# Order of side work in the feed-forward pairs of a fused attention and mixture kernel: silu before routing, later transpositions, remainders moved between VectorE and GpSimd

## The chip, the cores and the metric

The kernel runs on one core of a Trainium2 chip. The metric is the device time of one execution in microseconds (us); lower is better. Five engines have queues of their own: PE (TensorE, matrix products and transpositions), ACT (ScalarE), DVE (VectorE), POOL (GpSimd) and SP (here it only issues DMAs). Each works through its queue in order and waits on semaphores that the others raise.

## The reference

The input x is 2 x 1024 tokens of width 128, in float32. Four layers follow one another, each added to x behind a layer norm:

```python
x = x + attn_a(layernorm(x))   # 16 heads of differential attention, an rms norm per head, a projection
x = x + ffn(layernorm(x))
x = x + attn_b(layernorm(x))   # heads of 8, energies summed over positions, a softmax over 16, a projection
x = x + ffn(layernorm(x))      # the same weights as the first
```

with this feed forward, of 64 experts and one shared one:

```python
shared = silu(xf @ Ws_up) @ Ws_down
aff = xf @ centroids.T
_, idx = top_k(aff + expert_biases, 8)
w = sigmoid(take_along_axis(aff, idx)); w = w / (sum(w) + 1e-8)
cw = zeros(T, 64).at[rows, idx].add(w)
h = silu(einsum('td,edf->etf', xf, W_up))
routed = einsum('etd,te->td', einsum('etf,efd->etd', h, W_down), cw)
```

All 64 experts are computed for all tokens; the gates `cw` are zero for those that a token has not chosen.

## The kernel before

**Attention.** The first attention fills some 650 us. It is cut into 256 quads (`quad(s)`, s from 0 to NQ - 1 = 255): PE computes four score tiles of 128 x 512 (L1324) and, one quad later, the weighted sums of values in two halves (L1351); ACT takes the exponential of every score tile (L863). DVE finds row maxima 12 quads ahead and is done with them 12 quads before the end. In the last quads, side work for the first chunk of the feed forward is put between: `SIDE[NQ - 12]` to `SIDE[NQ - 4]`.

**Feed forward.** Tokens are taken in chunks of 512; n = 0 to 3 is the first feed forward, n = 4 to 7 the second. A chunk is 17 steps: w = 0 to 15 is a pair of blocks, each with two experts on the partitions, w = 16 the shared expert alone. Here (n, w) names a step, and g = 17 n + w counts them. In every product a float32 operand is split into a high part and a remainder, and three products are summed (L1449 to L1451). Of a pair g:

- PE: `up(g)`, six products of XH, XL with WUH, WUL, into two banks of PSUM;
- ACT: `silu(g)` (L948), in place;
- DVE: `gated(g)` (L1098) multiplies by the gates and writes HF;
- ACT: `high(g)` (L941) rounds HF to HH;
- DVE or POOL: `low(g)` (L1106 or L775), the remainder HL = HF - HH;
- PE: `down(g)`, six products that add up over the whole chunk in one bank.

In one step the queues hold, in this order:

```python
# PE                      ACT                    DVE                     POOL
side((n, w))              side((n, w))           side((n, w))            side((n, w))
up(g)                     silu(g)                gated(g)                low(g - 1), if low_on_pool(g - 1)
down(g - 3)               high(g - 1)            low(g - 1), if not on POOL
```

`up(g)` uses the banks of `up(g - 2)` again and so waits for `gated(g - 2)`. At w = 3, ACT also empties the sum of the chunk before (`chunk_sum`, L958, ahead of `side`), and PE's `down` of the new chunk's first pair waits for that. Which engine does `low(g)` is a rule, `low_on_pool(g)`, from what the side work of step g + 1 is. 44 of the 136 remainders are on POOL.

`SIDE` is the table of the side work: for each step a list of stages, each of which has a part on PE and parts on other engines. For a chunk of the feed forward they are: `stats` (DVE, L992, then the root on POOL, L621 and following), `norm` (DVE, L1004, writes XC), `x_T` (PE, L1230, transposes XC; ACT, L909 and L910, copies it to XT and XH; POOL, L745, makes XL), `affinity` (PE, L1407; ACT, L888, copies it, then L916 takes the sigmoid; POOL adds the biases), `top` (DVE), `sum` (DVE), `gate_T` (PE, L1411; ACT or, in the attention's last quads, DVE, L1127, copies it to CWT). For `gate_T` of chunk n SP then writes the gates to DRAM (L566), and reads them back, repeated over 64 partitions, two DMAs of 256 KB for a pair, into three slots of GATE (L577). The second attention is side work of the first feed forward too: `x_T` of "b", then `gram`, `gram_k`, `q_k`, `energy`, `soft_exp`, `mix_T`, `v_mix`, `v_all`, one stage a step. Its result goes out to DRAM and back through SP (`mix_out`, L552, at (3, 1) and (5, 1); `mix_back`, L558, at (3, 3) and (5, 3)), and `out_b` at (3, 5) and (5, 5) needs it.

In ACT's `side`, the stage `affinity` is a copy, a load of the table for sigmoid, the sigmoid, and later a load of the table for silu; there are seven such places in the feed forward, at (0, 9), (1, 9), (2, 0), (3, 10), (3, 16), (5, 10) and (5, 16).

Of the kernel before, what the change touches and what calls it, by code (L numbers as in the profile page):

```python
# [20 lines left out]
NCH = TOK // BANK  # L21
# [111 lines left out]
def ring_order(names):  # L133
# [19 lines left out]
SIDE = {  # L153

    NQ - 12: [("heads_T", 0)], NQ - 11: [("proj", 0), ("stats", ("f", 0))], NQ - 10: [("norm", ("f", 0))],
    NQ - 8: [("x_T", ("f", 0))], NQ - 7: [("affinity", 0)], NQ - 6: [("top", 0)], NQ - 5: [("sum", 0)], NQ - 4: [("gate_T", 0)],

    (0, 2): [("heads_T", 1)], (0, 4): [("proj", 1), ("stats", ("f", 1))], (0, 6): [("norm", ("f", 1))],
    (0, 8): [("x_T", ("f", 1))], (0, 9): [("affinity", 1)], (0, 11): [("top", 1)], (0, 13): [("sum", 1)],
# [18 lines left out]
for n, b in ((2, 0), (4, 1)):  # L178
    c, f = 2 * b + 1, 2 * b + NCH
    also((n, 4), ("y_T", n - 1), ("stats", ("b", c)))  # L180
    also((n, 6), ("norm", ("b", c)))
    also((n, 7), ("x_T", ("b", c)))
    also((n, 8), ("gram", b))
    also((n, 9), ("gram_k", b))
    also((n, 10), ("q_k", b))
    also((n, 11), ("energy", b))
    also((n, 12), ("soft_exp", b), ("soft_mix", b))
    also((n, 13), ("mix_T", b))
    also((n, 14), ("v_mix", b))
    also((n, 15), ("v_all", 2 * b))  # L190
# [101 lines left out]
def hybrid_layer(nc, x, w_qkv, w_proj, b_proj, lam_q1, lam_k1, lam_q2, lam_k2, sub_w,  # L292
                 w_q, w_k, w_v, w_o, b_o, cent, e_bias, ws_up, ws_down, w_up, w_down, out):
    ctx = ExitStack()
    with ctx:
# [151 lines left out]
        def _(sp):  # L447
# [102 lines left out]
            def mix_out(b):  # L550
                sp.wait_ge(*evacuated(("v_all", 2 * b + 1)))
                sp.dma_start(mixed_d[b].rearrange("i d a j -> (d a) i j"), VP[:]).then_inc(mix_w[b], 16)  # L552

            def mix_back(b):
                sp.wait_ge(mix_w[b], 16)
                if b:
                    sp.wait_ge(*evacuated(("out_b", 1)))
                sp.dma_start(RT[:], mixed_d[b].rearrange("i d a j -> (i d) (a j)")).then_inc(mix_r[b], 16)  # L558
# [10 lines left out]
            for n in range(2 * NCH):  # L569
                sp.wait_ge(gate_w, 16 * (n + 1))  # L570
                gates = gate_d[n].rearrange("(w u h) t -> w h u t", u=2, h=2)
                for w in range(FULL):
                    k = n * FULL + w
                    if k >= GSLOTS:
                        sp.wait_ge(hf_ok, k - GSLOTS + 1)
                    for h in range(2):
                        sp.dma_start(GATE[E * h:E * (h + 1), k % GSLOTS, :, :],  # L577
                                     gates[w, h].partition_broadcast(E)).then_inc(gate_ld[k % GSLOTS], 16)
                    if (n, w) in ((3, 1), (5, 1)):
                        mix_out((n - 3) // 2)  # L580
                    if (n, w) in ((3, 3), (5, 3)):
                        mix_back((n - 3) // 2)
# [212 lines left out]
        def _(act):  # L795
# [169 lines left out]
            for g in range(2 * NCH * WIDES):  # L965
# [572 lines left out]
```

## Time and profile before

| | us |
|---|---|
| median of 3 runs | 1110.72 |
| lowest and highest of them | 1108.67, 1111.96 |
| the profiled execution | 1112.18 |
| its span, first to last instruction | 1110.4 |

| engine | busy us | share of the span |
|---|---|---|
| PE | 1013.9 | 91% |
| DVE | 963.0 | 87% |
| ACT | 891.8 | 80% |
| POOL | 515.6 | 46% |

The profile is of one execution. Its clock of PE is at one of two levels: 1.00 is full speed (2.4 GHz), 0.50 half (1.2 GHz). In a timeline each row is one instruction or several alike: start, duration, engine, line, operation, tiles, sizes, count, and in brackets how long the engine was idle before it and what ended that. A matmul's row is longer than its share of PE, since matmuls overlap: starts are what counts.

### The profile page before, as it was taken

The page shows a single profiled execution, that of the slowest core. Times are in us where ns is not written, and L with a number is a line of the kernel's source. Part 1 is how long each engine was busy: PE and PEld are TensorE (multiplying, and loading weights), DVE is VectorE, ACT ScalarE, POOL GpSimd, SP SyncE. Part 2 cuts the span into 40 slices and gives each one's busy share as a digit, 9 for nine tenths or more (in the row PEclk, how much of TensorE's full clock was granted, in tenths as well). Part 3 has the DMA queues.
Part 4 walks back from the last instruction along what each step waited for, and adds up shares of the span by engine and source line. Part 5 has one row for each costly group of instructions (what it writes and reads, how often), then busy time and mean ns, then how long its engine had stood idle before and what let it go on. Part 6 is the DMA issues. An engine that isn't in the chain of part 4 may idle for free.

```text
span 1110.4 us, 21656 instructions
## 1 busy us (share of the span) xinstructions
PE 1013.9 (91%) x8016; PEld 517.5 (47%) x8016; DVE 963.0 (87%) x1174; ACT 891.8 (80%) x1466; POOL 515.6 (46%) x905
## 2 busy tenths in 40 slices
PE   6389999999999999999999999998899889999997
PEld 3022222222222223232322337776678667777875
DVE  7799999999999999999999738888868986687665
ACT  5189999999999999999999868767576767677765
POOL 3353556455645554455446645364325441442332
PEclk9579999999999999999999979999999999999999
DMA  8911110011001110111010026755567465857773
GB/s 279 302 33 36 51 49 24 29 51 50 25 27 51 50 31 22 51 50 31 23 51 21 3 68 166 175 135 135 143 155 187 114 171 138 209 142 176 190 194 86
DMA packets 80473, 108.91 MB, mean 98 GB/s; under 512 B 23536, under 2 KB 33520, under 8 KB 80368
## 3 DMA queue, kind: packets, MB, share of 16 engines
q1 hardware_dynamic: 70752, 103.07, 35.0%
q10 hardware_dynamic: 9616, 4.46, 1.5%
q8 instruction: 64, 1.05, 0.4%
q14 instruction: 41, 0.34, 0.1%
HBM read 95.57 MB, written 11.93 MB: 97 GB/s over the span
## 4 chain that ended last, share of the span: by engine, by line
DVE 57%; PE 22%; ACT 7%; issue 6%; DMA 5%; POOL 2%; SPq 1%; ACTq 0%; DVEq 0%; POOLq 0%
DVE NEGMAX L1057 46%; PE PS L1449 6%; PE PS L1451 5%; PE PS L1450 5%; DVE HF L1098 3%; DVE XC L1004 3%; DMA GATE<-gate_d 2%; PE PS L1351 2%; DVE HL L1106 2%; ACT HH L941 2%; PE PS L1324 1%; ACT PR L863 1%; ACT PS L948 1%; DVE ln_st L992 1%; DMA shift_d<-SHT 1%
## 5 line engine op out<-in xcount | busy, mean ns | idle before, releaser
L1057 DVE TENSOR_REDUCE NEGMAX<-PS 128x1 f32<-128x1024 f32 x512 | 585.0, 1211 | 9.7 <-PE PS L1287 9.1
L863 ACT ACTIVATE PR<-PS 128x512 f32<-128x512 f32 x1024 | 539.5, 601 | 42.4 <-PE PS L1324 30.3
L1351 PE MATMUL PS<-PR,VG 128*32 128x256 f32 (+1 forms) x3840 | 324.8, 410 | 16.7 <-ACT PR L863 1.3
L1324 PE MATMUL PS<-QB,KB 32*128 32x512 bf16 x1024 | 261.4, 390 | 3.7 <-DMA QB<-shift_d 2.3
L1287 PE MATMUL PS<-KA,QA 32*128 32x512 bf16 x1024 | 204.6, 397 | 30.3 <-DVE NEGMAX L1057 22.6
L1098 DVE TENSOR_TENSOR HF<-PS,GATE 128x1024 f32<-128x1024 f32 x128 | 156.1, 1221 | 71.0 <-ACT PS L948 70.6
L948 ACT ACTIVATE PS<-PS 128x1024 f32<-128x1024 f32 x128 | 129.3, 1010 | 91.7 <-PE PS L1451 90.5
L1324 PEld LDWEIGHTS PS<-QB,KB 32*128 32x128 bf16 x1024 | 75.2, 91 | 242.4 <-ACT PR L863 140.5
L775 POOL TENSOR_TENSOR HL<-HF,HH 128x1024 fp32r<-128x1024 f32 (+1 forms) x44 | 99.1, 2254 | 169.9 <-ACT HH L941 169.6
L941 ACT ACTIVATE HH<-HF 128x1024 fp32r<-128x1024 f32 (+1 forms) x136 | 139.7, 1028 | 26.9 <-DVE HF L1098 25.6
L1351 PEld LDWEIGHTS PS<-PR,VG 128*32 128x32 f32 x3840 | 76.7, 108 | 131.5 <-issue 65.9
L1106 DVE TENSOR_TENSOR HL<-HF,HH 128x1024 fp32r<-128x1024 f32 x92 | 116.3, 1265 | 21.6 <-ACT HH L941 21.2
L1449 PE MATMUL PS<-XH,WUH 128*128 128x512 f32 x256 | 108.9, 425 | 12.3 <-DVE HF L1098 12.3
L1449 PE MATMUL PS<-HH,WDH 128*128 128x512 f32 x256 | 103.5, 404 | 5.2 <-ACT YS L958 2.3
L1451 PE MATMUL PS<-XH,WUL 128*128 128x512 f32 x256 | 102.2, 399 | 0.0
L1450 PE MATMUL PS<-XL,WUH 128*128 128x512 f32 x256 | 101.9, 398 | 0.0
L1451 PE MATMUL PS<-HH,WDL 128*128 128x512 f32 x256 | 101.4, 396 | 0.0
L1450 PE MATMUL PS<-HL,WDH 128*128 128x512 f32 x256 | 101.2, 395 | 0.0
L683 POOL TENSOR_TENSOR ORC<-OSB,MINUS 128x16 f32<-128x16 f32 x32 | 93.1, 2910 | 9.9 <-DVE OSB L1083 7.6
L649 POOL TENSOR_TENSOR SHP<-NEGMAX,ZERO 128x16 bf16<-128x16 f32 x32 | 7.0, 217 | 168.8 <-DVE NEGMAX L1057 168.8
L1287 PEld LDWEIGHTS PS<-KA,QA 32*128 32x128 bf16 x1024 | 48.3, 91 | 58.5 <-DVE NEGMAX L1057 45.2
L1449 PEld LDWEIGHTS PS<-XH,WUH 128*128 128x128 f32 x256 | 48.9, 191 | 29.1 <-DVE HF L1098 18.6
(187 smaller groups left out, 991.4 us busy)
## 6 DMA issues: line engine op xcount, KB each, us to landing
GATE<-gate_d SPq DMA_DIRECT2D x256, 256.0 KB, 4.1
QA<-q_stack SPq DMA_DIRECT2D x64, 128.0 KB, 2.6
QB<-q_stack SPq DMA_DIRECT2D x16, 256.0 KB, 3.0
KB<-k_stack SPq DMA_DIRECT2D x16, 256.0 KB, 3.0
KA<-k_stack SPq DMA_DIRECT2D x60, 64.0 KB, 2.4
q_stack<-PARTS SPq DMA_DIRECT2D x12, 256.0 KB, 4.4
k_stack<-PARTS SPq DMA_DIRECT2D x12, 256.0 KB, 4.5
RAWU<-in_L_ffn_W_up_dram ACTq DMA_DIRECT2D x4, 512.0 KB, 13.3
```

The source lines that it names most:

```text
L863: nc.scalar.activation(PR[:, s % PRING, r, :], PS[:, SCORE_BANK[n], :], ACT.Exp, scale=SCALE_A).then_inc(p_ready, 1)
L941: nc.scalar.activation(HH[:, k, 0:u, :], HF[:, k, 0:u, :], ACT.Copy).then_inc(hh_ok, 1)
L948: nc.scalar.activation(PS[:, z:z + 2, :], PS[:, z:z + 2, :], ACT.Silu).then_inc(silu_ok, 1)
L1057: nc.vector.tensor_reduce(NEGMAX[:, hs % 2, col:col + 1], PS[:, e:e + 2, :].rearrange("p b n -> p (b n)"), axis=AX_X, op=ALU.max, negate=T ...
L1098: nc.vector.tensor_tensor(HF[:, k, :, :], PS[:, z:z + 2, :], GATE[:, h % GSLOTS, :, :], op=ALU.mult).then_inc(hf_ok, 1)
L1106: nc.vector.tensor_tensor(HL[:, k, 0:u, :], HF[:, k, 0:u, :], HH[:, k, 0:u, :].bitcast(F32), op=ALU.subtract).then_inc(hl_ok, 1)
L1287: last = mm(PS[:, e + h, :], QA[lo:lo + STRIP, u, r // 2, nt * P:(nt + 1) * P], KA[lo:lo + STRIP, u, r // 2, :], start=True, stop=True)
L1324: mm(PS[:, SCORE_BANK[n], :], KB[strip, u, mt * P:(mt + 1) * P], QB[strip, u, half * BANK:(half + 1) * BANK], start=True, stop=True).then_ ...
L1351: last = mm(PS[STRIP * r:STRIP * (r + 1), 7, cols], VG[:, u, mt, r // 2, :], PR[:, s % PRING, r, cols], start=mt == 0, stop=mt == TB - 1 a ...
L1449: mm(dst, ah, bh, start=first, stop=False)
L1450: mm(dst, ah, bl, start=False, stop=False)
L1451: return mm(dst, al, bh, start=False, stop=last)
```

## The change

1. `SIDE`: `gate_T` of chunk 0 goes from quad NQ - 4 to NQ - 2.
2. `SIDE`: `x_T` of chunk 3 goes from (1, 16) to (2, 0), and its `affinity`, `top`, `sum` and `gate_T` one step later each.
3. `SIDE`: for "b" chunks 1 and 3, `x_T` goes from (n, 7) to (n, 8), n = 2 and 4, and the ten stages behind it one step later each.
4. ACT: the routing part (copy and sigmoid of `affinity`) comes behind `silu(g)`, before `high(g - 1)`.
5. `mix_out` and `mix_back` are stages of `SIDE` now, issued by ACT at (n + 1, 0) and (n + 1, 2), and no longer by SP.
6. `low_on_pool`: the remainder that falls at an `affinity` step is always POOL's, and the last five are all DVE's. From before to now (0, 8), (1, 8), (2, 0), (3, 9), (3, 15), (5, 9) and (5, 15) go from DVE to POOL, and (2, 2), (7, 14) and (7, 16) from POOL to DVE.

```diff
-    NQ - 8: [("x_T", ("f", 0))], ..., NQ - 5: [("sum", 0)], NQ - 4: [("gate_T", 0)],
+    NQ - 8: [("x_T", ("f", 0))], ..., NQ - 5: [("sum", 0)], NQ - 2: [("gate_T", 0)],
...
-    also((n, 7), ("x_T", ("b", c)))
-    also((n, 8), ("gram", b))
+    also((n, 8), ("x_T", ("b", c)))
+    also((n, 9), ("gram", b))
...
-    also((n, 16), ("v_all", 2 * b + 1))
+    also((n + 1, 0), ("v_all", 2 * b + 1), ("mix_out", b))
+    also((n + 1, 2), ("mix_back", b))
...
 def low_on_pool(g):
-    n, w = divmod(g + 1, WIDES)
-    return g >= POOL_BUSY and (works((n, w), DVE_SIDE) and not works((n, w), POOL_SIDE) or not works((n, w), POOL_SIDE) and w % 3 == 0)
+    here = divmod(g + 1, WIDES)
+    if not POOL_BUSY <= g < 2 * NCH * WIDES - 5:
+        return False
+    if works(here, ("affinity",)):
+        return True
+    return not works(here, POOL_SIDE) and (works(here, DVE_SIDE) or here[1] % 3 == 0)
...
-            def side(where):
+            def side(where, routing=False):
                 for item in SIDE.get(where, ()):
                     stage, arg = item
                     bank = side_bank(item) if item in SIDE_ITEM else None
+                    if routing != (stage == "affinity" and item not in TAIL_SIDE):
+                        continue
...
+                    elif stage == "mix_out":
+                        act.wait_ge(*evacuated(("v_all", 2 * arg + 1)))
+                        act.dma_start(mixed_d[arg].rearrange("i d a j -> (d a) i j"), VP[:]).then_inc(mix_w[arg], 16)
+                    elif stage == "mix_back":
+                        act.wait_ge(mix_w[arg], 16)
+                        if arg:
+                            act.wait_ge(*evacuated(("out_b", 1)))
+                        act.dma_start(RT[:], mixed_d[arg].rearrange("i d a j -> (i d) (a j)")).then_inc(mix_r[arg], 16)
...
                 side((n, w))
                 if g > 1:
                     silu(g)
+                side((n, w), True)
                 if g:
                     high(g - 1)
```

What the queues hold at three places. **PE, the attention's last quads** (L1411, now L1413, is the transposition of the first gates), before:

```order
L1324 MATMUL PS<-QB,KB 128x512 x2
L1411 MATMUL PS<-ident,SQ 64x128 x4
L1351 MATMUL PS<-PR,VG 32x256 x4
L1324 MATMUL PS<-QB,KB 128x512 x2
L1351 MATMUL PS<-PR,VG 32x256 x4
L1324 MATMUL PS<-QB,KB 128x512 x2
L1351 MATMUL PS<-PR,VG 32x256 x4
L1324 MATMUL PS<-QB,KB 128x512 x2
L1351 MATMUL PS<-PR,VG 32x256 x4
L1324 MATMUL PS<-QB,KB 128x512 x2
```

and now:

```order
L1326 MATMUL PS<-QB,KB 128x512 x2
L1353 MATMUL PS<-PR,VG 32x256 x4
L1326 MATMUL PS<-QB,KB 128x512 x2
L1353 MATMUL PS<-PR,VG 32x256 x4
L1326 MATMUL PS<-QB,KB 128x512 x2
L1353 MATMUL PS<-PR,VG 32x256 x4
L1326 MATMUL PS<-QB,KB 128x512 x2
L1353 MATMUL PS<-PR,VG 32x256 x4
L1326 MATMUL PS<-QB,KB 128x512 x2
L1413 MATMUL PS<-ident,SQ 64x128 x4
L1353 MATMUL PS<-PR,VG 32x256 x4
```

Both begin at the same pair of score tiles; four halves of weighted values with their scores now come ahead of the transposition.

**ACT, steps (0, 8) to (0, 10)** (PS<-PS is a silu, HH<-HF a high, SQ the routing), before:

```order
L948 ACTIVATE PS<-PS 128x1024
L941 ACTIVATE HH<-HF 128x1024
L888 ACTIVATE SQ<-PS 128x256
L916 ACT_TABLE_LOAD
L916 ACTIVATE SQ<-SQ 128x256
L948 ACT_TABLE_LOAD
L948 ACTIVATE PS<-PS 128x1024
L941 ACTIVATE HH<-HF 128x1024
L948 ACTIVATE PS<-PS 128x1024
```

and now:

```order
L949 ACTIVATE PS<-PS 128x1024
L942 ACTIVATE HH<-HF 128x1024
L949 ACTIVATE PS<-PS 128x1024
L879 ACTIVATE SQ<-PS 128x256
L909 ACT_TABLE_LOAD
L909 ACTIVATE SQ<-SQ 128x256
L942 ACTIVATE HH<-HF 128x1024
L949 ACT_TABLE_LOAD
L949 ACTIVATE PS<-PS 128x1024
```

The silu of the step goes ahead of the routing, and the table for silu is loaded again only behind the high.

**DVE, the last steps of chunk 7**, before:

```order
L1098 TENSOR_TENSOR HF<-PS,GATE 128x1024
L1106 TENSOR_TENSOR HL<-HF,HH 128x1024
L1098 TENSOR_TENSOR HF<-PS,GATE 128x1024
L1106 TENSOR_TENSOR HL<-HF,HH 128x1024
L1137 TENSOR_TENSOR X<-X,PS 128x512
```

and now:

```order
L1100 TENSOR_TENSOR HF<-PS,GATE 128x1024
L1108 TENSOR_TENSOR HL<-HF,HH 128x1024
L1100 TENSOR_TENSOR HF<-PS,GATE 128x1024
L1108 TENSOR_TENSOR HL<-HF,HH 128x1024 x2
L1108 TENSOR_TENSOR HL<-HF,HH 128x512
L1139 TENSOR_TENSOR X<-X,PS 128x512
```

Two remainders, of (7, 14) and (7, 16), stand on DVE that were POOL's.

## Rows read from the trace of the kernel before

**Rows 1.** Page, section 1: busy us (share) and instructions

```profile
PE 1013.9 (91%) x8016; PEld 517.5 (47%) x8016; DVE 963.0 (87%) x1174; ACT 891.8 (80%) x1466; POOL 515.6 (46%) x905
```

**Rows 2.** Timeline of chunk 7: two silus, and what PE waited for

```profile
1093.39 1.01 ACT L948 ACTIVATE PS<-PS 128x1024 f32<-128x1024 f32 x1 [0.81 <-PE PS L1451]
...
1096.17 1.01 ACT L948 ACTIVATE PS<-PS 128x1024 f32<-128x1024 f32 x1 [0.81 <-PE PS L1451]
```

**Rows 3.** Timeline of the last quads: ACT, then PE

```profile
641.72 5.35 ACT L863 ACTIVATE PR<-PS 128x512 f32<-128x512 f32 x10 [0.33 <-PE PS L1324]
...
647.65 1.03 PE L1411 MATMUL PS<-ident,SQ 128*64 128x128 f32 x4 [1.70 <-POOL SQ L760]
...
658.92 0.80 PE L1449 MATMUL PS<-XH,WUH 128*128 128x512 f32 x1
```

**Rows 4.** Windows: length, busy us (count) by engine, PE's clock, DMA share, GB/s

```profile
647.20:660.86 13.66, 13.21 (x77) 4.14 (x78) 0.68 (x1) 7.79 (x13) 8.79 (x19) 0.50 0.57 125
...
797.39:800.80 3.41, 3.41 (x11) 2.73 (x10) 0.63 (x1) 1.00 (x2) 0.86 (x1) 0.50 0.32 92
...
913.44:916.85 3.41, 1.62 (x9) 1.44 (x10) 2.78 (x3) 0.60 (x1) 2.60 (x2) 1.00 0.27 72
```

**Rows 5.** Timeline from the first gates to the first gated pair: DVE, SP

```profile
648.72 0.68 DVE L1127 COPY CWT<-PS 64x512 f32<-64x512 f32 x1 [1.91 <-PE PS L1411]
663.13 1.22 DVE L1098 TENSOR_TENSOR HF<-PS,GATE 128x1024 f32<-128x1024 f32 x1
...
651.69 0.61 SPq L577 DMA_DIRECT2D GATE<-gate_d  x1
```

**Rows 6.** Tile GATE, 648 to 672 us: landing of its 13 loads

```profile
DMA to landing us min/median/max: 3.5/4.3/6.2
```

**Rows 7.** Timeline of (2, 6) to (2, 8), then (4, 7): DVE and PE

```profile
793.73 3.16 DVE L1004 TENSOR_SCALAR XC<-X,ln_mv,ln_inv 128x128 f32<-128x128 f32 x4
...
797.03 0.77 PE L1230 MATMUL PS<-ident,XC 128*128 128x128 f32 x4 [3.52 <-DVE XC L1004]
...
803.56 0.48 PE L1449 MATMUL PS<-XH,WUH 128*128 128x512 f32 x1
...
915.23 0.63 PE L1230 MATMUL PS<-ident,XC 128*128 128x128 f32 x4 [3.51 <-DVE XC L1004]
```

**Rows 8.** Timeline of the end of chunk 7: POOL, DVE, PE

```profile
1098.22 4.62 POOL L775 TENSOR_TENSOR HL<-HF,HH 128x1024 fp32r<-128x1024 f32 x2 [5.94 <-ACT HH L941]
...
1099.91 1.78 DVE L1106 TENSOR_TENSOR HL<-HF,HH 128x1024 fp32r<-128x1024 f32 x1 [1.48 <-ACT HH L941]
...
1100.75 0.47 PE L1449 MATMUL PS<-HH,WDH 128*128 128x512 f32 x1 [1.13 <-POOL HL L775]
```

**Rows 9.** Timeline of (0, 9) and (0, 11): ACT, DVE, POOL

```profile
686.72 0.38 ACT L888 ACTIVATE SQ<-PS 128x256 f32<-128x256 f32 x1
...
688.40 0.42 ACT L916 ACTIVATE SQ<-SQ 128x256 f32<-128x256 f32 x1
688.84 1.28 ACT L948 ACT_TABLE_LOAD   x1
690.13 1.01 ACT L948 ACTIVATE PS<-PS 128x1024 f32<-128x1024 f32 x1
...
697.60 1.22 DVE L1098 TENSOR_TENSOR HF<-PS,GATE 128x1024 f32<-128x1024 f32 x1
...
700.05 2.41 POOL L775 TENSOR_TENSOR HL<-HF,HH 128x1024 fp32r<-128x1024 f32 x1 [1.55 <-ACT HH L941]
```

**Rows 10.** Timeline of (2, 3): PE behind the chunk's sum

```profile
781.56 0.50 PE L1449 MATMUL PS<-HH,WDH 128*128 128x512 f32 x1 [0.46 <-ACT YS L958]
```

**Rows 11.** Timeline of (5, 10): ACT

```profile
982.40 0.36 ACT L888 ACTIVATE SQ<-PS 128x256 f32<-128x256 f32 x1
...
985.81 1.01 ACT L948 ACTIVATE PS<-PS 128x1024 f32<-128x1024 f32 x1
```

**Rows 12.** Line L552, the mixed values to DRAM, issued twice by SP

```profile
DMA to landing us min/median/max: 4.1/4.1/4.2
```

More of the change, by code:

```diff
@@ L155 @@
     NQ - 12: [("heads_T", 0)], NQ - 11: [("proj", 0), ("stats", ("f", 0))], NQ - 10: [("norm", ("f", 0))],
-    NQ - 8: [("x_T", ("f", 0))], NQ - 7: [("affinity", 0)], NQ - 6: [("top", 0)], NQ - 5: [("sum", 0)], NQ - 4: [("gate_T", 0)],
+    NQ - 8: [("x_T", ("f", 0))], NQ - 7: [("affinity", 0)], NQ - 6: [("top", 0)], NQ - 5: [("sum", 0)], NQ - 2: [("gate_T", 0)],
     (0, 2): [("heads_T", 1)], (0, 4): [("proj", 1), ("stats", ("f", 1))], (0, 6): [("norm", ("f", 1))],
@@ L163 @@
     (1, 10): [("heads_T", 3), ("x_T", ("b", 0))], (1, 11): [("top", 2)], (1, 12): [("proj", 3), ("stats", ("f", 3))],
-    (1, 13): [("sum", 2)], (1, 14): [("norm", ("f", 3))], (1, 15): [("gate_T", 2)], (1, 16): [("x_T", ("f", 3))],
-    (2, 0): [("affinity", 3)], (2, 2): [("top", 3)], (2, 4): [("sum", 3)], (2, 6): [("gate_T", 3)],
+    (1, 13): [("sum", 2)], (1, 14): [("norm", ("f", 3))], (1, 15): [("gate_T", 2)],
+    (2, 0): [("x_T", ("f", 3))], (2, 1): [("affinity", 3)], (2, 3): [("top", 3)], (2, 5): [("sum", 3)], (2, 7): [("gate_T", 3)],
     (4, 1): [("top", 5)], (4, 3): [("sum", 5)], (4, 5): [("gate_T", 5)],
@@ L181 @@
     also((n, 6), ("norm", ("b", c)))
-    also((n, 7), ("x_T", ("b", c)))
-    also((n, 8), ("gram", b))
[L184 to L190, printed above, removed]
-    also((n, 16), ("v_all", 2 * b + 1))
+    also((n, 8), ("x_T", ("b", c)))
+    also((n, 9), ("gram", b))
+    also((n, 10), ("gram_k", b))
+    also((n, 11), ("q_k", b))
+    also((n, 12), ("energy", b))
+    also((n, 13), ("soft_exp", b), ("soft_mix", b))
+    also((n, 14), ("mix_T", b))
+    also((n, 15), ("v_mix", b))
+    also((n, 16), ("v_all", 2 * b))
+    also((n + 1, 0), ("v_all", 2 * b + 1), ("mix_out", b))
+    also((n + 1, 2), ("mix_back", b))
     also((n + 1, 4), ("y_T", n))
@@ L548, in _ @@
             rows_out = out.rearrange("b (n p) c -> p (b n) c", p=P)
[L550 to L558, printed above, removed]
             def store(c):
@@ L578, in _ @@
                                      gates[w, h].partition_broadcast(E)).then_inc(gate_ld[k % GSLOTS], 16)
[L579 to L582, printed above, removed]
                     if n > NCH and w == 9:
```

## The prediction

> **What bounds the kernel now.** I read the engines' shares first [rows 1]: four engines are busy half of the time or more and none always, so the stages have to be told apart. The reader is to see in it only that PE leads. The change touches nothing ahead of the last quads, so I went on to the timeline behind 640 us.
>
> In chunk 7, which has almost no side work, silus start 2.78 us apart and each waits for PE [rows 2]: twelve products, 0.232 each. That is PE's own pace, and ACT has 0.81 to spare in each pair. Of eight chunks of 16 pairs and one shared step (2.78 and 1.39, half the products) this makes 367 us; from the first product at 658.92 [rows 3] to the last pair's DVE work near 1101.7 [rows 8] there are 443. The 76 between are waits, and the question is which of them the change takes away and which it makes. I looked at every wait of PE over 1 us there.
>
> **The first gates (part 1).** In quad 252 PE comes to the transposition of the gates and sits idle 1.70 us, until POOL has them at 647.5 [rows 3]. Behind it PE's clock is 0.50 for 13.66 us [rows 4]: from 647.65 to the first product at 658.92, 11.27 for one transposition, seven halves of weighted values with their scores, and the start [rows 3]. Ahead of it the exponentials set the pace, ten in 5.35 us, so 0.535 each and 2.14 for a quad of four [rows 3]. Two quads later the gates are long there. PE then comes to the transposition at 645.95 + 2 x 2.14 = 650.2, and to `up(0)` at 645.95 + 3.5 x 2.14 + 0.6 for the transposition = 654.0, 4.9 earlier. But the gates themselves are later by 2.2: the copy to CWT ended at 649.40 and the first load was issued at 651.69 [rows 5]; its pair's second one, 0.6 behind, takes the median of 4.3 [rows 6], so it lands at 656.6, and now at 658.8. `gated(0)` started at 663.13 [rows 5]; silu is no limit (654.0 + 1.4 + 1.3 for the table), so it starts at 658.9. **Term: -4.2.** The wait that goes is followed by another, for GATE. Bounds: if the clock falls all the same, only the idle 1.7 is saved; if GATE were there, 4.9 and the half-speed loss in `up(0)`, 1.0: -1.7 to -5.9.
>
> **Transpositions behind norms (part 3).** At (2, 7) PE waits 3.52 for the norm, which DVE does from 793.73 to 796.89, late and long, and at (4, 7) 3.51 [rows 7]. Now step (2, 7) has no such wait: `up(2, 7)` and `down(2, 4)` fill 793.5 to 796.3, PE then transposes at 797.0, and `up(2, 8)` waits for `gated(2, 6)`, which ends 1.2 behind the norm: 798.1. With 1.4 for `up` and 1.4 for `down` it is 800.9, and the gram products take 1.7: `up(2, 9)` at 802.6. Before, `up(2, 8)` was at 803.56 [rows 7], `up(2, 9)` 3.0 later at 806.6. **-4.0.** A part of it is the clock: behind the wait PE ran at 0.50 for 3.41 us [rows 4], which costs half of that, 1.7, and PE idle only 0.7 and 0.5 should not bring it about. At (4, 7) the clock stayed at 1.00 through an idle time as long [rows 4], so the same sum gives **-2.4**. Bounds for both together: nothing but the clock, -1.7, or both whole waits and the clock, -8.7. The ten stages behind follow in the same order one pair later and cost the same.
>
> **The last remainders (part 6).** PE waits 1.13 for POOL, whose two remainders take 4.62 together; DVE's own between them is stretched to 1.78 [rows 8]. On DVE the remainder of (7, 14) can follow `gated(7, 15)` at 1098.4 and end at 1099.6, where PE had come to at about 1099.6. Those of (7, 15) and (7, 16), 1.2 and 0.7, then keep ahead of PE. **-1.1**, between -0.5 and -1.1.
>
> **Routing behind silu (parts 2, 4 and 6).** Before, routing took ACT from 686.72 to 690.13: copy, load, sigmoid, load, and the sigmoid's end at 688.82 is 1.31 ahead of the silu, that is one load of 1.28 [rows 9]. ACT's work is the same now; what is new is that `silu(g)` can't start before PE has ended `up(g)`, while routing could. At (0, 9), ACT is free at 686.7 and `up` ends at 687.8: 1.1 idle put in. Then silu to 688.8, copy, load, sigmoid to 690.9, high to 691.9, load, and silu (0, 10) at 693.15, where it was 692.0. `gated(0, 9)` gains 2.2 and PE only 0.45, for it had waited no more. `high(0, 8)` comes as before, but its remainder is now POOL's, 2.41 long [rows 9] for DVE's 1.22: ready 694.4, PE wanted it 693.4. `gated(0, 10)` is late by 0.75, and so, through `top`, is `gated(0, 11)`, which was at 697.60 [rows 9] and set PE there. **+0.8.**
>
> At (2, 1), where routing of chunk 3 now stands, it is dearer. It used to run at (2, 0), when ACT had nothing else. Now ACT comes late to (2, 3), where it must empty chunk 1's sum: from silu (2, 1), which by the same replay of the queues from (1, 14) on starts at 775.7, follow silu, routing without the last load 2.1, high, load 1.3, silu and high, four of them at 0.94, so the copy of the sum starts at 782.9 and ends 783.45; PE waited for it until 781.56 [rows 10]. That is 1.9, and DVE has one more remainder in its full stretch to (2, 6), that of (2, 2), +0.5. **+2.4.** The move of `x_T` itself brings nothing, since PE waited right behind it for `gated` too. At (5, 10) PE runs at half speed when ACT has its copy at 982.40 [rows 11], `up` ends at 983.9, and 1.5 of idle ACT are put in, all of which DVE, full until `gated(5, 12)`, hands on: **+1.6**. The other four have 0.5 idle or a norm of DVE in the same place: 0.2 each, **+0.8**. Together **+5.6**; bounds 0 (DVE's relief pays for it) and 2.4 in each of the seven, 16.8.
>
> For the table loads the row decides: no gap beside the 1.28. The Trainium skill (ScalarE: Activation LUTs, What ACT_TABLE_LOAD costs) has some 1.38 of drain more at each switch. By it routing ahead of the high would be 1.4 longer, and the sum 7 x 1.4 = 9.8 higher, +3.7. The rows of before have no place for it, so it gets no chance.
>
> **The two DMAs on ACT's queue (part 5).** Written at (3, 0) and read at (3, 2): the write lands 4.1 after issue [rows 12] and 5.6 lie between, so ACT does not wait; issuing hides in the 0.81 of a pair. 0; at most +1.5 if the write took 7.
>
> **Sum.** -4.2 - 4.0 - 2.4 - 1.1 + 5.6 = -6.1. The profiled execution took 1112.18, so it would take 1106.1; it lies 1.46 above the median of 1110.72, and against that the forecast is **1104.6**. A measurement of this kernel can tell some 0.3%, 3.3 us, from no change.
>
> **Rivals.**
> *A. Routing costs nothing.* DVE has seven remainders fewer in its full stretches, which may pay for later silus. For: `gated` comes 2.2 earlier at (0, 9). Against: DVE idles there, so relief is worth little. Price: -11.7 + 0.6 = -11.1, 1099.6.
> *B. The gates are late.* PE, idle before the first gates land, falls to half speed, or six loads at once take the longest landing, 6.2 for 4.3 [rows 6]. Then -4.2 becomes -1.7 and the sum -3.6 or less, say 1108. For: 13.66 us at 0.50 followed an idle 1.7 [rows 4]. Against: 3.5 idle at (4, 7) brought nothing.
> *C. Remainders on POOL hold up DVE's.* DVE's took 1.78 in place of 1.22 beside POOL's [rows 8]; at seven places 0.56 each, +3.9, gives -2.2, 1108.5. The Trainium skill (SBUF — State Buffer, SBUF: two separate sides) says it outright: GpSimd and a DVE operation with two SBUF inputs lock each other out for the whole instruction. The row agrees.
> *D. Slower: `down` behind routing.* At every routing step PE waits for POOL's remainder or the chunk's sum as at (2, 1), 2.4 in each of seven, 16.8, and falls to half speed at two of them, 2 x 1.7. Then +20.2 - 11.7 = +8.5, 1119. It decides from 1.7 per place upward. For: I found 2.4 and 1.6 at two. Against: three had little.
> *E. It does not do what it says*: the order of the queues shows it done; no chance of its own.
>
> **How the numbers follow.** Forecast 0.46, and within it 1101.5 to 1107.5; A 0.20, B 0.13, C 0.11, D 0.10. Slower by over 0.3%: D's most, 0.09. Faster: A, 0.38 of the forecast, 0.09 of B and C, so 0.67. The same: the rest, 0.24. The range takes in A and reaches up to B and C: 1098.5 to 1110.0, with D and the ends left out.
>
> **What would show it.** PE's clock stays at 1.00 from 645 to 657 and `gated(0)` starts near 659, released by GATE; no wait over 1 us at x_T in (2, 8) and (4, 8); none for POOL at the end; a new wait of PE of 2 to 3 us at (2, 3), for YS; silu (g + 1) at routing steps 1 us later against its neighbours. I am wrong if the clock falls in the last quads all the same, or if the seven places sum to under 2 or over 9 us.

## The result and the profile after

| | kernel before | changed kernel |
|---|---|---|
| median us, 16 runs each | 1111.62 (1106.88 to 1114.34) | 1108.68 (1106.24 to 1111.91) |
| ratio | 1 | 0.9973, interval 0.9961 to 0.9984 |
| profiled execution us (span) | 1112.18 (1110.4) | 1111.91 (1110.0) |

The ratio makes 3.0 us less (1.8 to 4.3), where 6.1 less was forecast; the range held the time. It is just inside 0.3%, the forecast's bound of "the same". The profiled execution of the changed kernel was the slowest of its 16, so the two spans differ by 0.4 only. A second profile of it, e12, has a span of 1104.4, and a second one of the kernel before, e11, has 1109.4. What follows leans on both pairs. Two single runs, one of e1 at 1465 us and one of e4 at 2873 us, took far longer than all others and stand in no ratio.

Page of the changed kernel, section 1, for [rows 1]:

```profile
PE 1011.8 (91%) x8016; PEld 519.5 (47%) x8016; DVE 958.6 (86%) x1170; ACT 891.6 (80%) x1466; POOL 521.5 (47%) x909
```

Seven subtractions have gone from DVE to POOL and three back, four in all (1174 and 905 before). The shares tell nothing else; the places do.

**The last quads and the first gates.** Timeline of the changed kernel, PE, then SP's queue and DVE (start, us, engine and operation, in brackets the idle time before it and what ended it):

```profile
651.53 0.63 PE L1413 MATMUL PS<-ident,SQ 128*64 128x128 f32 x4
654.44 0.50 PE L1451 MATMUL PS<-XH,WUH 128*128 128x512 f32 x1
...
661.54 0.66 PE L1232 MATMUL PS<-ident,XC 128*128 128x128 f32 x4 [2.42 <-DVE OSB L1085]
...
655.15 9.69 SPq L572 DMA_DIRECT2D GATE<-gate_d  x10
...
660.04 1.23 DVE L1100 TENSOR_TENSOR HF<-PS,GATE 128x1024 f32<-128x1024 f32 x1 [2.18 <-DMA GATE<-gate_d]
```

Windows of the changed kernel (columns as in [rows 4]): the last quads, the first products, and behind the two waits of the next fence:

```profile
647.20:660.86 13.66, 11.35 (x106) 5.04 (x104) 2.96 (x6) 10.69 (x18) 9.27 (x20) 1.00 0.36 86
662.43:665.84 3.41, 3.41 (x9) 2.69 (x9) 2.29 (x2) 1.78 (x3) 3.06 (x5) 0.50 1.05 227
768.25:771.66 3.41, 3.41 (x12) 2.72 (x11) 1.99 (x1) 1.90 (x4) 2.28 (x1) 0.50 1.05 230
785.31:788.72 3.41, 3.41 (x12) 2.72 (x11) 3.34 (x14) 0.76 (x1) 0.73 (x1) 0.50 0.56 154
```

The idle 1.70 and the long half clock of [rows 3, 4] are gone, and the first product comes at 654.44, not 658.92. But the first load is issued at 655.15 (651.69 in [rows 5]), DVE sits until 660.04 and is released by GATE, PE idles 2.42, and a half clock of 3.41 us follows, where the kernel before had none.

**The chunk's sum at (2, 3), and the step before.** Timeline of the changed kernel, PE and ACT:

```profile
766.97 0.50 PE L1451 MATMUL PS<-XH,WSUH 128*128 128x512 f32 x1 [2.26 <-DVE HF L1100]
784.24 0.50 PE L1451 MATMUL PS<-HH,WDH 128*128 128x512 f32 x1 [2.98 <-ACT YS L959]
...
783.60 0.59 ACT L959 ACTIVATE YS<-PS 128x512 f32<-128x512 f32 x1
```

The wait for YS was 0.46 in [rows 10]; the forecast said 2 to 3, and it is 2.98. Behind each of these two waits stands a window at 0.50.

**Norms, mixed values, end.** Timeline of the changed kernel: the norm and the transpositions behind it in chunks 2 and 4; MIX; the last remainders.

```profile
796.84 3.20 DVE L1006 TENSOR_SCALAR XC<-X,ln_mv,ln_inv 128x128 f32<-128x128 f32 x4
800.19 0.63 PE L1232 MATMUL PS<-ident,XC 128*128 128x128 f32 x4 [0.73 <-DVE XC L1006]
914.93 0.63 PE L1232 MATMUL PS<-ident,XC 128*128 128x128 f32 x4 [0.78 <-DVE XC L1006]
...
823.44 1.22 DVE L1108 TENSOR_TENSOR HL<-HF,HH 128x1024 fp32r<-128x1024 f32 x1
824.58 0.28 DVE L1191 COPY MIX<-PS 128x128 f32<-128x128 f32 x1
825.01 0.46 PE L1439 MATMUL PS<-MIX,WVT 128*128 128x128 f32 x2 [0.54 <-DVE MIX L1191]
...
1098.97 1.22 DVE L1108 TENSOR_TENSOR HL<-HF,HH 128x1024 fp32r<-128x1024 f32 x1
1100.52 1.83 DVE L1108 TENSOR_TENSOR HL<-HF,HH 128x1024 fp32r<-128x1024 f32 x2 [0.34 <-ACT HH L942]
```

PE's waits of 3.52 and 3.51 for the norms [rows 7] have become 0.73 and 0.78, and the wait of 1.13 for POOL at the end [rows 8] is gone. New is MIX: its copy stands behind a whole remainder of DVE, and PE waits for it. In the kernel before the copy followed the gated product directly, and PE did not wait. One stage earlier, at MIXT, PE waits longer too. There a small operation of DVE, which scales the softmax (EN), runs beside a remainder of POOL. Timeline of the changed kernel: POOL, DVE, PE.

```profile
818.50 2.39 POOL L766 TENSOR_TENSOR HL<-HF,HH 128x1024 fp32r<-128x1024 f32 x1 [6.56 <-ACT HH L942]
820.39 0.53 DVE L1186 TENSOR_SCALAR EN<-EN,en_r 128x16 f32<-128x16 f32 x1
821.39 0.30 PE L1436 MATMUL PS<-ident,MIXT 128*128 128x128 f32 x1 [0.80 <-DVE MIXT L1187]
```

The same places of the kernel before, DVE and PE:

```profile
818.13 0.23 DVE L1184 TENSOR_SCALAR EN<-EN,en_r 128x16 f32<-128x16 f32 x1
820.05 1.22 DVE L1098 TENSOR_TENSOR HF<-PS,GATE 128x1024 f32<-128x1024 f32 x1 [1.35 <-ACT PS L948]
821.19 0.28 DVE L1189 COPY MIX<-PS 128x128 f32<-128x128 f32 x1
...
818.84 0.30 PE L1434 MATMUL PS<-ident,MIXT 128*128 128x128 f32 x1 [0.50 <-DVE MIXT L1185]
821.76 0.39 PE L1437 MATMUL PS<-MIX,WVT 128*128 128x128 f32 x2
```

The scaling takes 0.53 in place of 0.23, and ends as POOL's remainder does (820.92 and 820.89). So the waits grew by 0.3 at MIXT and 0.5 at MIX.

**The ledger.** To add such places up I took, in each profile, the start of every silu, counted from the first MAX8 behind 600 us (at 641.06 in the profile of before), so that what the long attention part does from one execution to the next is out. Each column is the time from one silu to the next one named, less the mean of the two profiles of before (which are within 0.27 us of that mean in each):

```
to silu          0,8   0,13   1,13    2,6    2,9    3,0    4,6    4,9    5,0   5,14    7,0    end    sum
changed         -4.5   +1.4   +0.8   +3.6   -3.5   +1.0   -0.5   -2.2   +1.0   +1.5   +0.5   -1.0   -2.0
e12, the same   -4.5   +1.4   +0.7   +1.9   -3.3   +1.0    0.0   -2.3   +1.0   +0.3   +0.5   -1.9   -5.3
e10             +0.1   +0.9   +0.7   +0.8   +0.9    0.0   -0.5   +1.4    0.0   +1.4   +0.5   -1.1   +5.1
e7              -4.9    0.0    0.0    0.0   -3.8   +0.9    0.0   -2.3   +1.0   -0.3    0.0   -1.0  -10.4
e13             -6.0    0.0    0.0    0.0    0.0    0.0    0.0    0.0    0.0   -0.3    0.0   -0.3   -6.6
e15             -4.3   +1.4   +0.7   +1.9   -3.3   +0.2   -0.6   -2.2   +0.3   +1.4   +0.5   -1.9   -6.1
e9              -6.5   +0.3   +0.4   -0.3   -3.8   +0.2   +1.1   -3.9   +0.2   +0.1   +1.0   -1.9  -13.2
e14             -6.3   +1.4   +2.0   +3.6   -3.5   +0.9   -0.6   -2.2   +1.0   +1.3   +0.5   -1.0   -3.0
e4              -4.0   +1.4   +1.2   +3.6   -3.5   +0.9   -0.4   -2.2   +1.0   +0.3   +0.4   -1.9   -3.2
e2              -4.2   +1.3   +0.7   +0.8   -3.8   +0.9   -0.6   -2.2   +1.0   +0.9   +0.4   -1.9   -6.8
e3              -4.5   +0.4   +0.4   +0.4   -3.0   +0.9   +1.0   -3.9   +1.0   -1.0   +1.0   -1.9   -9.2
e5              -4.3   +0.3   +0.5   -0.3   -3.8   +0.9   +1.1   -3.9   +1.0   +0.1   +1.0   -1.9   -9.4
e1              -4.2   +0.3   +0.7   -0.8    0.0    0.0    0.0    0.0    0.0   +0.1    0.0    0.0   -3.8
e8              -0.2    0.0   +0.7   -0.7    0.0    0.0    0.0    0.0    0.0   -0.2    0.0   -1.3   -1.6
e16             -6.6   +0.3   +0.7   -0.8   -3.8   +0.2    0.0   -2.2   +0.2   -0.3    0.0   -1.9  -14.1
```

Most places that a kernel leaves alone read 0.0 to a few hundredths. There are three exceptions. Where a half clock of 3.41 us stands near 740 us (e1, e8, e16), (1, 13) reads +0.7 and (2, 6) gives it back, and e1 has +0.3 at (0, 13). (5, 14) moves by 0.3. And the end column moves by 1.0 in e7 and e10, which have nothing changed there: from silu (7, 0) to DVE's last addition to X all profiles with the old remainders take 51.9 us and all with the last five on DVE 51.0, but from that addition to the end it is 3.4 us in eleven profiles and 4.1 to 4.5 in seven. Both profiles of the kernel before are among the seven; the changed kernel has 4.3 and, in e12, 3.4.

### The profile page after: what moved, and what is told of

It reads as the page before. It is cut to its first block, busy times and chain, and to the rows that moved or that the text cites. A ratio compares the mean times of both kernels' runs of the same rounds, so it can differ in the third digit from the quotient of the medians.

```text
span 1110.0 us, 21656 instructions
## 1 busy us (share of the span) xinstructions
PE 1011.8 (91%) x8016; PEld 519.5 (47%) x8016; DVE 958.6 (86%) x1170; ACT 891.6 (80%) x1466; POOL 521.5 (47%) x909
## 4 chain that ended last, share of the span: by engine, by line
DVE 56%; PE 26%; ACT 6%; issue 5%; DMA 5%; SPq 1%; ACTq 0%; POOL 0%; DVEq 0%
DVE NEGMAX L1059 46%; PE PS L1451 7%; PE PS L1453 6%; PE PS L1452 6%; DVE HF L1100 3%; DMA GATE<-gate_d 2%; DVE XC L1006 2%; PE PS L1353 2%; DVE HL L1108 2%; ACT PR L854 2%; ACT PS L949 1%; PE PS L1326 1%; ACT HH L942 1%; ACT L949 1%; DVE ln_st L994 1%
## 5 line engine op out<-in xcount | busy, mean ns | idle before, releaser
L766 POOL TENSOR_TENSOR HL<-HF,HH 128x1024 fp32r<-128x1024 f32 (+1 forms) x48 | 109.0, 2270 | 163.1 <-ACT HH L942 162.8
L1108 DVE TENSOR_TENSOR HL<-HF,HH 128x1024 fp32r<-128x1024 f32 x88 | 109.9, 1249 | 9.8 <-ACT HH L942 9.3
```

Of the source, the lines that this page charges most:

```text
L1108: nc.vector.tensor_tensor(HL[:, k, 0:u, :], HF[:, k, 0:u, :], HH[:, k, 0:u, :].bitcast(F32), op=ALU.subtract).then_inc(hl_ok, 1)
```

## Experiments

Every ratio is against the kernel before on the same chip, with its 95% interval.

**First gates later, alone (e1), on the kernel before.**

```
-    NQ - 5: [("sum", 0)], NQ - 4: [("gate_T", 0)]
+    NQ - 5: [("sum", 0)], NQ - 2: [("gate_T", 0)]
```

> The kernel before with one edit: the first gates are transposed at quad NQ-2 instead of NQ-4. Theory 1 (the trace of the changed kernel: first silu 4.97 us earlier, but a new half-clock stretch of 3.4 us after PE's wait for the first GATE loads): about 2 us faster than before, ratio near 0.998, first silu near 656.5, the half clock of 13.66 us in the last quads gone and a new one of 3.4 us behind it. Theory 2 (the forecast's term): 4.2 us faster, ratio 0.996, no new half clock before chunk 1. Theory 3: the clock's stretch only moves and the gain is gone by chunk 2: within 0.5 us of before.

0.9986 (0.9967 to 1.0004), 1.6 us. The profile has the first silu 6.4 us earlier in the ledger's frame, a new half clock of 3.41 us at 660.2, and 3.8 in all. That is theory 1 in kind, and its size as far as the interval reaches.

**Parts of the change undone, each on the changed kernel (e2, e3, e4, e5).** e2 puts pair 3 back, e3 the order on ACT, e4 the remainders; e5 is e2 and e3 together.

```
e2:
-    (2, 0): [("x_T", ("f", 3))], (2, 1): [("affinity", 3)], (2, 3): [("top", 3)], (2, 5): [("sum", 3)], (2, 7): [("gate_T", 3)],
+    (1, 16): [("x_T", ("f", 3))],
+    (2, 0): [("affinity", 3)], (2, 2): [("top", 3)], (2, 4): [("sum", 3)], (2, 6): [("gate_T", 3)],
e3:
                 side((n, w))
+                side((n, w), True)
                 if g > 1:
                     silu(g)
-                side((n, w), True)
e4:
-    if works(here, ("affinity",)):
-        return True
```

> The changed kernel with x_T(f,3) back at (1,16), affinity, top, sum and gate transposition of 3 back at (2,0), (2,2), (2,4), (2,6). Theory 1 (the place at (1,14) to (2,6) costs 4 to 5 us, waits of 2.4 us at up(1,16) and 3.2 us for YS at (2,3) with a half clock behind each): 7 to 8 us faster than before, ratio near 0.993. Theory 2 (the forecast's +2.4 for that place): 5.4 us faster, ratio 0.995. Theory 3 (the late sigmoid costs the same wherever it stands, and the place is not the cause): as the changed kernel, 3 us faster, 0.997.

> The changed kernel with the routing's copy and sigmoid ahead of the silu of their step again, as before the change, all else kept. Theory 1 (what the change gives back comes from the silu standing ahead of copy and sigmoid): the +0.3 at (0,9), the +4 to +5 at (2,1) to (2,4) and the +1.8 at (5,10) are gone; 8 to 9 us faster than before, ratio near 0.992. Theory 2 (it comes from the remainders that POOL now makes beside the routing, for which down waits 0.86 to 1.23 us): as the changed kernel, 3 us faster. Theory 3 (the forecast's prices): 5.6 us better than the changed kernel's forecast of -6.1 stood, that is the changed kernel's measured -3.0 less 5.6: 8.6 faster.

> The changed kernel with the remainders of the routing's steps back on DVE, all else kept. Theory 1 (POOL's remainder of 4.6 us is too late for the down projection at (0,11) and (3,11), which waited 1.23 and 0.86 us for it): 1 us better than the changed kernel, 4 us faster than before, ratio 0.9964. Theory 2 (DVE, which makes top and sum and the gated products there, is the tighter engine): 1 to 2 us worse than the changed kernel, ratio 0.999. Theory 3: neither is late enough to matter, 0.9973.

> The changed kernel with both undone: pair 3's routing at its old steps, and copy and sigmoid ahead of the silu. What stays of the change: first gates later, pair steps and their DMAs later, remainders by the new rule. Theory 1 (the two undone parts cost one place, (2,1) to (2,4), with its half clocks, and the sigmoid at (5,10) and (0,9) besides; their undoing hardly adds up): 6 us faster than before, ratio 0.9945, as each alone gave 1.5 and 2.2 us over the changed kernel. Theory 2 (they add up in full): 6.7 us or more, 0.994 or less. Theory 3 (the shift of pair 3 only costs with the sigmoid behind the silu; ahead of it the shift is free): as e3_routing_ahead, 5.2 us, 0.9957.

e2: 0.9965 (0.9952 to 0.9979), 3.9 us, between theories 2 and 3; the place at (2, 6) fell from +3.6 to +0.8. e3: 0.9957 (0.9943 to 0.9971), 4.8, between theories 1 and 2. e4: 0.9984 (0.9970 to 0.9998), so the remainders on POOL at the routing's steps cost nothing that shows (between theories 2 and 3). e5: 0.9927 (0.9910 to 0.9943), 8.1 us, which is 5.1 below the changed kernel where e2 and e3 had 0.9 and 1.8. So it is theory 2. Whether the two add up to more than their sum is not shown: each of these differences is uncertain by about 2 us, and the ledger says the contrary. There e3 alone is 9.2 better than before and e5 9.5, and in column (2, 6), where the changed kernel loses 2.9 in the mean, either part undone leaves 0.8 or 0.4. The 9.2 of e3's profile is more than its 12 runs bear out; one profile shows one execution.

**POOL's remainders in another phase (e6 on e5, e15 on the changed kernel).**

```
-    return not works(here, POOL_SIDE) and (... or here[1] % 3 == 0)
+    return not works(here, POOL_SIDE) and (... or here[1] % 3 == (here[0] in (2, 4) and here[1] > 8))
```

> As e5, and in chunks 2 and 4 behind step 8 POOL makes the remainders of steps 10, 13, 16 in place of 9, 12, 15. Theory 1 (the pair steps, moved one on, now have their copy of MIX behind a remainder on DVE, for which PE waits 0.71 us at v_mix, and silu (3,0) and (5,0) come 0.9 us late each): silu (3,0) and (5,0) no longer lose 0.9 us, 1.8 us faster than e5 in the trace. Theory 2 (the 0.9 us is VP's copy and its transfer at step (n+1,0)): no change against e5.

> The changed kernel with the POOL remainders of chunks 2 and 4 behind step 8 at steps 10, 13, 16. Theory 1 (the +0.9 at v_mix twice): 1.8 us faster than the changed kernel, 4.8 faster than before, ratio 0.9957, silu (3,0) and (5,0) without their 0.9 us. Theory 2 (e6's gain over e5 was noise or needs the routing ahead): 0.997.

e6: 0.9910 (0.9891 to 0.9929), 1.9 us below e5. e15: 0.9959 (0.9945 to 0.9974), 1.6 below the changed kernel. The intervals overlap with those of e5 and of the changed kernel; the places decide. In the ledger the two columns "3,0" and "5,0" fall from +1.0 to +0.2 and +0.3. Timeline of e15 at the same step:

```profile
819.54 2.41 POOL L766 TENSOR_TENSOR HL<-HF,HH 128x1024 fp32r<-128x1024 f32 x1 [8.39 <-ACT HH L942]
819.67 0.28 DVE L1191 COPY MIX<-PS 128x128 f32<-128x128 f32 x1
...
820.24 0.38 PE L1439 MATMUL PS<-MIX,WVT 128*128 128x128 f32 x2
...
821.55 1.48 DVE L1108 TENSOR_TENSOR HL<-HF,HH 128x1024 fp32r<-128x1024 f32 x1
```

The remainder is POOL's, the copy is no longer behind it, and PE does not wait. At MIXT the scaling of EN is back at 0.23 and PE's wait at 0.50. Theory 1 holds, and e6's theory 2 (VP and its transfer) has at most the 0.2 and 0.3 that are left.

**Pair steps later, alone (e7), and last remainders on DVE, alone (e8), on the kernel before.** e7 is the change's own hunk for `x_T` and the ten stages, with the transfers on ACT. e8:

```
-    return g >= POOL_BUSY and (
+    return POOL_BUSY <= g < 2 * NCH * WIDES - 5 and (
```

> The kernel before with one part: x_T of the pair 2b+1 and the ten steps behind it one step later, with the mix transfers issued by ACT. Theory 1 (trace of the changed kernel): -3.8 at (2,8) and -2.3 at (4,8), +0.9 at (2,14) and (4,14): 4.3 us faster than before, ratio 0.996. Theory 2 (the forecast): -6.4, ratio 0.994. Theory 3 (the gains are half clocks that show in the one profile and only move): under 2 us by the medians, 0.998 to 0.9995.

> The kernel before with one part: the last five remainders on DVE. Theory 1: PE waits 0.26 us in place of 1.13 for the last remainder, 1 us faster, ratio 0.999. Theory 2 (DVE becomes late for the gated products of the last steps): no gain.

e7: 0.9958 (0.9940 to 0.9976), 4.7 us; the ledger has -3.8, +0.9, -2.3, +1.0. Theory 1. e8: 0.9990 (0.9978 to 1.0002), 1.1 us, so by the times the sign is likely and not certain. The trace has 0.9, as in every profile with these remainders on DVE.

**Routing behind silu, alone (e10), on the kernel before**: e3's move the other way round.

> The kernel before with one part: copy and sigmoid of the routing in chunks 0 to 6 behind the silu of their step. Theory 1 (as e3_routing_ahead shows by its undoing): 2.2 us slower than before, ratio 1.002, with 1.8 us at (5,10) and under 0.5 at each other place, pair 3's step (2,0) included. Theory 2 (the forecast's prices): 5 us slower, 1.0045. Theory 3 (it costs something only where pair 3 has been moved): (5,10) alone, 1 us or less, 1.001.

1.0029 (1.0014 to 1.0043), 3.2 us slower, between theories 1 and 2. It isn't (5, 10) alone: the ledger has seven columns of 0.5 to 1.4. In two of them, (2, 9) and (4, 9), there is no routing; a half clock is longer there (6.83 us at 797) or new (at 917).

**One quad earlier (e9 on e6, e13 on the kernel before, e14 on the changed kernel)**: `("gate_T", 0)` at NQ - 3.

> As e6, with the first gates transposed at quad NQ-3 instead of NQ-2. Theory 1 (at NQ-2 PE waits for the first GATE loads behind the first up projections, with a half clock of 3.4 us behind it, which costs 3 of the 6 us by which the first silu is earlier; one quad earlier POOL's SQ is there in time and the loads land 1.2 us sooner): first silu as in e6, and 1 to 3 us faster than e6, ratio 0.989. Theory 2 (a quad earlier PE waits for SQ again, with the half clock of the kernel before): 1 to 2 us slower than e6, 0.9925. Theory 3: no difference, 0.991.

> The kernel before with one edit: first gates at quad NQ-3. Theory 1 (the forecast's 4.2 us are there to be had, and NQ-2 loses them in the wait for the first GATE loads): 4 to 5 us faster than before, ratio 0.996, first gated product 1.0 to 1.6 us behind silu (0,0) as before, no half clock in the last quads or at the first products. Theory 2 (the gain of e9 over e6 came with other parts of it): as e1, 1.6 us, 0.9986.

> The changed kernel with its first gates at NQ-3 instead of NQ-2. Theory 1: 3 us faster than the changed kernel, so 6 us faster than before, ratio 0.9945, which is the forecast's time. Theory 2 (the two half clocks at (1,16) and (2,3) take it back): 0.997.

e9: 0.9877 (0.9855 to 0.9898), 13.7 us. e13: 0.9957 (0.9943 to 0.9970), 4.8, where NQ - 2 had 1.6. e14: 0.9955 (0.9940 to 0.9970), 5.0, 2.0 below the changed kernel. Timeline of e13:

```profile
648.70 0.63 PE L1411 MATMUL PS<-ident,SQ 128*64 128x128 f32 x4
653.89 0.50 PE L1449 MATMUL PS<-XH,WUH 128*128 128x512 f32 x1
...
652.32 7.36 SPq L577 DMA_DIRECT2D GATE<-gate_d  x8
...
657.22 1.21 DVE L1098 TENSOR_TENSOR HF<-PS,GATE 128x1024 f32<-128x1024 f32 x1
```

Its window there:

```profile
647.20:660.86 13.66, 12.54 (x108) 6.42 (x107) 4.52 (x8) 11.51 (x19) 10.90 (x20) 1.00 0.59 134
```

The transposition has no wait for POOL, the loads are issued 1.57 ahead of the first product (0.71 behind it in the changed kernel), and DVE no longer waits for GATE. The first silu is at the same 14.07 behind the mark as with NQ - 2; what NQ - 2 lost, it lost behind it. The products behind that wait were at half clock in eight of nine profiles with NQ - 2; with NQ - 3 none of four had a half clock there.

**The same kernels again (e11, e12).**

> The kernel before once more, for a second profile. Theory 1 (which waits of PE are followed by a half clock differs from one execution to the next): first silu 2 to 5 us from the first profile's, the 13.66 us stretch of the last quads absent or in another place, one or two of the later stretches gone or new. Theory 2 (they belong to the program): the same five stretches within 1 us.

> The changed kernel once more, for a second profile. Theory 1 (as for the kernel before): stretches of half clock at other waits than in the first profile, silu (2,4) less than 4.3 us late against before, and a span nearer 1107 than 1110 us. Theory 2: the same six stretches within 1 us, silu (2,4) 4 us late.

e11: the same stretches, each 1.4 us sooner like all of the execution, so theory 2. e12: theory 1, with one stretch near 780 where the first profile had two (768, 785), and one near 862 in place of those at 741 and 980. The first of the two waits of PE in the timeline of e12:

```profile
764.60 0.51 PE L1451 MATMUL PS<-XH,WSUH 128*128 128x512 f32 x1 [2.26 <-DVE HF L1100]
```

Its window there:

```profile
765.88:769.29 3.41, 3.41 (x18) 2.83 (x17) 2.02 (x1) 2.84 (x5) 2.99 (x2) 1.00 1.09 227
```

and e7, which has the last quads of the kernel before, in the timeline there:

```profile
647.78 0.60 PE L1406 MATMUL PS<-ident,SQ 128*64 128x128 f32 x4 [1.70 <-POOL SQ L747]
655.07 0.50 PE L1444 MATMUL PS<-XH,WUH 128*128 128x512 f32 x1
```

Its window there:

```profile
645.00:660.00 15.00, 12.21 (x114) 5.28 (x114) 3.75 (x8) 11.28 (x20) 9.83 (x20) 1.00 0.50 114
```

An idle of 2.26 was followed by 0.50 in one execution and by 1.00 in the other, and so was the idle 1.70 for POOL.

**Remainders of the routing's steps on DVE, on e9 (e16)**: e4's edit.

> As e9, with the remainders of the routing's steps on DVE. Theory 1 (with the sigmoid ahead of the silu, POOL's remainder is the last to be ready: PE waits 1.47 us for it at (6,1), 0.77 at (0,11)): 1 to 2 us faster than e9, ratio 0.9865. Theory 2 (as between the changed kernel and e4, DVE has no room for it): 0 to 1 us slower than e9, 0.988.

0.9887 (0.9867 to 0.9906), median 1099.01 for e9's 1099.10: no difference, so neither theory's 1 us shows; the interval would hide 1 us.

## Why the forecast was off, step by step

**First gates, -4.2: right for the profile, too much for the median.** The ledger has -4.5, and -4.3 in the mean of the four profiles of this program's start (the changed kernel, e4, e12, e15). The waits came as told, one for POOL going and one for GATE coming. Two errors cancelled, which is luck: the first silu came 6.4 earlier and the first product 5.9, not 4.9, and the products behind the wait for GATE fell to half speed, which I had left to rival B (priced at -1.7, since I took its gain to be lost whole). But "behind it PE's clock is 0.50" also took a stretch that some executions lack for a property of the program. Of the five profiles with the old place four have it and e7 has not, and there the first silu is 4.6 us earlier. Counted as four in five, -4.3 is -3.4 for a median. e1 gave 1.6 (3.7 faster to 0.4 slower).

**Transpositions behind norms, -4.0 and -2.4: right**, -3.4 and -2.2 in the mean.

**"The ten stages behind follow in the same order one pair later and cost the same": this step failed.** They cost 1.0 us twice. The order of the stages is the same, but the rule that deals remainders to POOL goes by the step's number (every third), and did not move with them. So at `mix_T` POOL's remainder now runs beside DVE's scaling of EN, 0.53 in place of 0.23, and PE waits 0.80 in place of 0.50; and the copy of MIX stands behind a remainder of DVE, for which PE waits 0.54. e15 changed that rule alone: both waits are as before, the two columns fall from 1.9 to 0.5, and the time by 1.6. In the ledger no other term is off by as much.

**Last remainders, -1.1: right**, 0.9 in every profile that has them; e8's time gives 1.1 (2.4 faster to 0.2 slower).

**Routing behind silu, +5.6: right as a sum, within it not.** Undoing it and pair 3's shift together gave 5.1 back (e5), and the part alone on the kernel before cost 3.2 (e10). (2, 1) was +2.4 and measured +3.6, +3.6, +3.6, +1.9 and +1.9 in the five profiles that have it, 2.9 in the mean: the wait for YS is the same in e12, 2.97, and one half clock more or less is the difference. (5, 10) was +1.6 and measured between +0.3 and +1.5. Too low were (0, 9), +0.8 for 1.4, and (1, 9), "0.2 each" for 0.7, which e12 has without any half clock there. POOL's remainder, which the forecast made late for PE at (0, 9), has no share that shows: e4, without it, has the same 1.4.

**Two DMAs on ACT, 0**: not tried by itself. With e15's rule the two columns in which their steps lie have +0.2 and +0.3 left.

**The sum.** By the means of the columns over the changed kernel, e4, e12, e14 and e15, each where it has the place unchanged, it is -4.3 + 1.4 + 1.0 + 2.9 - 3.4 + 1.0 - 0.4 - 2.2 + 1.0 + 1.0 + 0.5 - 1.5 = -3.0, and -2.1 with the old start as four in five. 3.0 was measured, 1.8 to 4.3. That the two agree to the digit is chance: of the -1.5 at the end only 0.9 is the change's, the rest is the stretch behind the last addition, in which both profiles of before are long. Without it the sum is -2.4, or -1.5 with the old start as four in five. Against -6.1 the ten stages account for 1.9, (0, 9), (1, 9) and (2, 1) for 1.9 together, the norms for 0.8; the rest, -1.5, is (5, 10), the late places of chunks 3 and 5 and the end, which came out better than forecast, the end by that stretch.

**Rivals.** A (routing costs nothing) falls by e5 and e10. B (the gates are late) came half true: PE's clock fell behind the wait for GATE, but in the profiles the start still gains 4.3 and not 1.7. C (POOL's remainders hold up DVE's) falls as a price at the routing's steps: taking them from POOL gains nothing (e4, e16). A DVE remainder beside POOL's does take 1.48 instead of 1.22 in e15's rows, so the effect that the Trainium skill states (SBUF — State Buffer, SBUF: two separate sides) is there. What such a delay costs depends on whether PE waits for DVE at that moment: at the seven places nothing shows, at `mix_T`, where DVE scales EN beside POOL's remainder, it is 0.3 us twice. D (2.4 at every routing step) falls: only (2, 1) reached it. The 1.38 us of drain at a table switch that the Trainium skill gives (ScalarE: Activation LUTs, What ACT_TABLE_LOAD costs) is absent in the new order too. Timeline of the changed kernel at (0, 9), ACT and PE:

```profile
688.41 1.04 ACT L942 ACTIVATE HH<-HF 128x1024 fp32r<-128x1024 f32 x1
689.48 1.28 ACT L949 ACT_TABLE_LOAD   x1
690.77 1.01 ACT L949 ACTIVATE PS<-PS 128x1024 f32<-128x1024 f32 x1
...
692.06 0.47 PE L1451 MATMUL PS<-HH,WDH 128*128 128x512 f32 x1 [1.06 <-POOL HL L766]
```

From the end of `high` at 689.45 to the silu there are 1.32 us, the load's 1.28 among them.

**Open.** What decides whether a wait is followed by half clock was not settled; the runs show only that the same wait goes either way. That the medians show somewhat less than the ledger in most experiments fits the one profile in five without the long stretch, and was argued, not shown. The granted clocks of the unprofiled runs fit it. The stretch of 13.66 us at 0.50 lowers the mean clock of a run by 0.006. The two profiles of the kernel before have 0.970 and 0.971; of 94 runs of it beside the experiments 20, about one in five, have 0.975 or more, and their median is 2.4 us lower than that of the other 74. Of e7's seven runs only the profiled one has 0.980, at 1102.25 us; the others have 0.972 to 0.974, at 1106.4 to 1109.0.

**The version that beats both** is e9: first gates at NQ - 3, pair steps later, last five remainders on DVE, routing where and how it was but with the remainders of its steps on POOL, POOL's phase moved with the pair steps, the mixed values' two DMAs on ACT. 1099.1 us, 0.9877 of the kernel before. e16 does as well.

## What to carry to other kernels

When a chain of stages is moved by one step, list every rule that goes by the step's number and ask which of them stays behind; here a copy of 0.28 us behind a remainder of 1.22 and a scaling held up by 0.3 beside POOL cost 1 us, twice. At a join between two phases a stage can come too early or too late, as at the one join tried here: take the latest place at which what it starts (here the GATE loads) is still issued ahead of its first user, and try the neighbours. Take the price of a half clock from several profiles, and weigh it by how often it is there.

## What the hardware showed that I had not expected

The same idle time of PE (1.70 for POOL, 2.26 for DVE) was followed by a granted clock of 0.50 in one execution and 1.00 in another, with nothing changed in the program ahead of it; one such stretch of 13.7 us made the first silu come 20.4 instead of 15.8 us behind the mark. Nearly all else repeats: between the two profiles of the kernel before every column of the ledger but one (0.5 at (5, 14)) agrees within 0.1 us, while the mark at their start lies between 639.5 and 643.8 us in the 18 profiles of all kernels. So an effect of 1 us that a time of 1110 hides can be read from the place, if half clocks are kept apart from it.

DVE's scaling of EN, 128 x 16 numbers, took 0.23 us in all 20 cases where POOL was idle and 0.53 in all 16 where POOL's remainder was under way, over the 18 profiles with two chunks each, and then ended within 0.05 us of the end of POOL's remainder.
